# Second attention: one tile's projections, turns and relay moved one step forward on every engine

## What is computed

```python
q = (x @ Wq.T).reshape(B, S, 32, 16).transpose(0, 2, 1, 3)
k = _split_kv(x @ Wk.T, B, S)
v = _split_kv(x @ Wv.T, B, S)
q = q * cos + rotate_half(q) * sin
k = k * cos + rotate_half(k) * sin
scores = einsum('bhqd,bhkd->bhqk', q, k) / sqrt(16)
allowed = (j <= i) & (j > i - 128)
attn = softmax(where(allowed, scores, -inf))
out = einsum('bhqk,bhkd->bhqd', attn, v) @ Wo.T
x = layernorm(x + out)
```

## Time and profile before

| | |
|---|---|
| runs | 726.03, 734.14, 737.02 us (median 734.14) |
| the profiled execution | 728.87 us, its span 727.1 us |
| busy | PE 616.0 us (85%), DVE 393.3 (54%), ACT 270.3 (37%), POOL 238.9 (33%) |
| mean granted clock of TensorE | 0.911 |
| chain that ended last | PE 62%, DVE 10%, ACT 9%, DMA 7% |

### The profile page before, as it was taken

How to read it: one execution, slowest core, us unless ns; L and a number is a source line. 1 busy time by engine, 2 the same in 40 slices (tenths; PEclk the granted TensorE clock), 3 DMA queues, 4 the chain that set the end, 5 groups by cost and what they waited for, 6 DMA issues and landing times.

```text
span 727.1 us, 13453 instructions
## 1 busy us (share of the span) xinstructions
PE 616.0 (85%) x5108; PEld 482.4 (66%) x5108; DVE 393.3 (54%) x1126; ACT 270.3 (37%) x433; POOL 238.9 (33%) x348
## 2 busy tenths in 40 slices
PE   2998999669889787989989895868789799999984
PEld 2987976557667555666767673645458688888761
DVE  4325445697765774757777484552554243323264
ACT  5155045366654223334344342444430122221213
POOL 6002523543410245535444452362007311111071
PEclk9999999889999885999999897577799899999997
DMA  8921211342056425536272648020007759998465
GB/s 293 394 115 31 52 33 26 104 134 74 0 139 150 119 96 81 132 46 159 45 152 89 88 119 156 2 89 2 1 1 283 270 209 416 418 417 292 168 165 182
DMA packets 49455, 104.37 MB, mean 144 GB/s; under 512 B 12208, under 2 KB 18480, under 8 KB 47856
## 3 DMA queue, kind: packets, MB, share of 16 engines
q1 hardware_dynamic: 30032, 61.68, 24.0%
q0 software_dynamic: 13744, 31.61, 19.3%
q10 hardware_dynamic: 5616, 10.23, 3.9%
HBM read 63.77 MB, written 35.13 MB: 136 GB/s over the span
## 4 chain that ended last, share of the span: by engine, by line
PE 62%; DVE 10%; ACT 9%; issue 7%; DMA 7%; POOL 4%; SPq 1%; POOLq 0%; ACTq 0%; DVEq 0%
PE bank L332 20%; PE bank L515 10%; PE bank L368 9%; ACT FP L1451 4%; DVE FP L914 3%; PE bank L601 3%; PE bank L586 3%; PE bank L573 3%; DMA QS<-QS 2%; PE bank L750 2%; POOL FP L1866 2%; PE bank L716 2%; PE bank L391 2%; PE bank L546 1%; PE bank L379 1%
## 5 line engine op out<-in xcount | busy, mean ns | idle before, releaser
L1451 ACT ACTIVATE FP<-bank 128x512 f32<-128x512 f32 (+1 forms) x244 | 138.6, 611 | 311.3 <-PE bank L586 128.6
L1184 DVE CUSTOM_DVE_ANT_0 kraw<-bank,maskb 128x256 bf16<-128x256 f32 (+1 forms) x256 | 88.5, 401 | 58.0 <-PE bank L573 58.0
L515 PE MATMUL bank<-W,XR 128*128 128x512 f32 x348 | 104.1, 444 | 0.2
L332 PE MATMUL bank<-FP 128*128 128x128 f32 x558 | 87.3, 311 | 0.8 <-ACT FP L1451 0.8
L368 PE MATMUL bank<-W,XR 128*128 128x512 f32 x288 | 76.6, 415 | 5.2 <-DVE W L914 5.2
L515 PEld LDWEIGHTS bank<-W,XR 128*128 128x128 f32 x348 | 69.4, 211 | 16.0 <-DVE XR L914 0.8
L1818 POOL TENSOR_SCALAR_AFFINE_SELECT FP<-FP 128x512 f32<-128x512 f32 x64 | 41.4, 669 | 114.8 <-ACT FP L1451 114.8
L368 PEld LDWEIGHTS bank<-W,XR 128*128 128x128 f32 x288 | 63.7, 271 | 11.3 <-DVE W L914 5.6
L332 PEld LDWEIGHTS bank<-FP 128*128 128x128 f32 x558 | 65.1, 192 | 2.8 <-DVE FP L914 1.6
L332 PE MATMUL bank<-RP,W 128*128 128x512 f32 x192 | 48.8, 413 | 5.0 <-issue 2.8
L914 DVE TENSOR_TENSOR FP<-FP,bank 128x128 f32<-128x128 f32 (+1 forms) x39 | 14.4, 369 | 70.5 <-ACT FP L1451 44.9
(11 more groups left out here) (168 smaller groups left out, 1019.1 us busy)
## 6 DMA issues: line engine op xcount, KB each, us to landing
FP<-in_experts_dram SPq DMA_DIRECT2D x31, 768.0 KB, 6.6
slots_out<-QS SPq DMA_DIRECT2D x48, 256.0 KB, 2.6
FP<-slots_in POOLq DMA_DIRECT2D x31, 256.0 KB, 6.6
slots_out<-FP ACTq DMA_DIRECT2D x31, 256.0 KB, 7.7
slots_in<-RP SPq DMA_DIRECT2D x7, 1024.0 KB, 13.1
RP<-slots_out POOLq DMA_DIRECT2D x16, 384.0 KB, 5.7
QS<-slots_out POOLq DMA_DIRECT2D x10, 384.0 KB, 8.3
FP<-in_shared_dram SPq DMA_DIRECT2D x4, 768.0 KB, 8.0
```

The source lines that it names most:

```text
L332: mm = nc.tensor.matmul(bank, lhs, rhs, start=(n == 0), stop=(n == len(terms) - 1))
L515: mm = nc.tensor.matmul(b[:, :], *terms[n], start=(n == 0), stop=(n == len(terms) - 1))
L1184: ins = nc.vector.tensor_tensor_reduce(masked[:, 2 * (f % 2) + m, 0:n], b[:, m, :], maskb[:, m0:m0 + n], 1.0, -BIG, ALU.add, ALU.max, hmax ...
L1451: return nc.scalar.activation(o, i, func, **kw)
```

## The change

Each engine's order is changed, and nothing else. TensorE: the Q projection goes to step 0, and the K projection of tile t + 1 into step 7 of the iteration before; `turn_maxima(i, 1)` goes from step 1 to step 0; the turn of rotated K from 2 to 1, of rotated Q from 3 to 2, the V projection from steps 2 and 3 to 1 and 2; `turn_x(t + 1)` from step 6 to step 3. VectorE: `maxima_out(i, 1)` goes to step 0 and ahead of `rotate(t, 1)` and `rope_sum(t, 1)`, which go to step 0 too; the second rotation goes to step 1, the low parts to steps 1 and 2, the low part of the next x to step 3. ScalarE and GpSimd follow. SP is the same.

```diff
--- before.py
+++ after.py
@@ -641,16 +641,18 @@
                         key_scores(i, 2 * (s // 2), s % 2)
                     if s < 2 and d >= 0:
                         context_rows(U, d, s)
-                    if s < 2 and 2 <= t < T:
-                        project2(t, 1 - s)
-                    if s == 1 and i >= 0:
+                    if s == 0 and 2 <= t < T:
+                        project2(t, 0)
+                    if s == 0 and i >= 0:
                         turn_maxima(i, 1)
-                    if s == 2 and 2 <= t < T:
+                    if s == 1 and 2 <= t < T:
                         turn_rotated(t, 1)
                         project2(t, 2, 0, DC)
-                    if s == 3 and 2 <= t < T:
+                    if s == 2 and 2 <= t < T:
                         project2(t, 2, DC, 2 * DC)
                         turn_rotated(t, 0)
+                    if s == 3 and 2 <= t < T - 1:
+                        turn_x(t + 1)
                     if s == 4 and d >= 0:
                         turn_context(U, U, d)
                     if (i, s) == (-1, 0):
@@ -667,10 +669,10 @@
                         output(U, R, d, 0, DC)
                     if s == 6 and d >= 0:
                         output(U, R, d, DC, DC)
-                    if s == 6 and 2 <= t < T - 1:
-                        turn_x(t + 1)
                     if s == 7 and d >= 0:
                         output(U, R, d, 2 * DC, DC)
+                    if s == 7 and 1 <= t < T - 1:
+                        project2(t + 1, 1)
                     if i >= 0 and s in (3, 5, 7):
                         weigh(i, s // 2 - 1)
                 if i == T - 1:
@@ -1252,21 +1254,23 @@
                         row_maxima(r, s)
                     if s < 2 and d >= 0:
                         context_divided(U, d, s)
-                    if s == 1 and 2 <= t < T:
+                    if s == 0 and i >= 0:
+                        maxima_out(i, 1)
+                    if s == 0 and 2 <= t < T:
                         rotate(t, 1)
                         rope_sum(t, 1)
-                    if s == 1 and i >= 0:
-                        maxima_out(i, 1)
-                    if s == 2 and 2 <= t < T:
+                    if s == 1 and 2 <= t < T:
                         parts_low(t, 1)
                         rotate(t, 0)
                         rope_sum(t, 0)
+                    if s == 2 and 2 <= t < T:
+                        parts_low(t, 0)
                     if s == 3 and r < T:
                         maxima_split(r, 0)
                     if (i, s) == (-1, 3):
                         low_dense(("x2", 2), xa[2][1], xa[2][0])
-                    if s == 3 and 2 <= t < T:
-                        parts_low(t, 0)
+                    if s == 3 and 2 <= t < T - 1:
+                        low_dense(("x2", t + 1), xa[t + 1][1], xa[t + 1][0])
                     if s == 4 and d >= 0:
                         low_dense(("co", d), ca[1], ca[0])
                     if i == -1 and s in (2, 4, 5, 6):
@@ -1275,8 +1279,6 @@
                         maxima_out(r, 0)
                     if (i, s) == (-1, 6):
                         rates(slice(G, T), 4)
-                    if s == 6 and 2 <= t < T - 1:
-                        low_dense(("x2", t + 1), xa[t + 1][1], xa[t + 1][0])
                     if s == 7 and r < T:
                         maxima_split(r, 1)
                     if s == 7 and d >= 0:
@@ -1642,11 +1644,13 @@
                         context_out(d, 1)
                     if i >= 0 and (step % 2 == 0 or i >= 1):
                         weights_out(i, 2 * (step // 2), step % 2)
+                    if step == 1 and 2 <= t < T:
+                        parts_out_high(t, 1)
                     if step == 2 and 2 <= t < T:
-                        parts_out_high(t, 1)
-                    if step == 3 and 2 <= t < T:
                         values_out(t, ("qkv", t, 0))
                         parts_out_high(t, 0)
+                    if step == 3 and 2 <= t < T - 1:
+                        high_dense(("x2", t + 1), x2T[t + 1][:, 0])
                     if step == 4 and d >= 0:
                         high_dense(("co", d), coT[:, 0])
                     if (i, step) == (-1, 0):
@@ -1662,8 +1666,6 @@
                         high_part(15, 3, raw_c[3], wc_in[3])
                     if step == 6 and i >= 0:
                         context_out(i, 0)
-                    if step == 6 and 2 <= t < T - 1:
-                        high_dense(("x2", t + 1), x2T[t + 1][:, 0])
                     if i == T - 2 and step in (2, 5):
                         shared_high(step // 3)
                     if i == T - 1 and step == 2:
@@ -1838,11 +1840,11 @@
                         nc.gpsimd.memset(kS[:, 3].bitcast(F32), -1.0).then_inc(minus_ready, 1)
                     if i >= 0 and (step % 2 == 0 or i >= 1):
                         mask(i, 2 * (step // 2), step % 2)
-                    if step == 2 and i >= 0:
+                    if step == 1 and i >= 0:
                         stack_maxima(i, 1)
+                    if step == 3 and 2 <= t < T:
+                        stack_rows(t, 1)
                     if step == 4 and 2 <= t < T:
-                        stack_rows(t, 1)
-                    if step == 5 and 2 <= t < T:
                         stack_rows(t, 0)
                     if step == 6 and r < T:
                         stack_maxima(r, 0)
```

## The result

The changed kernel takes 749.66 us (747.16 to 752.93) against 734.92 us (726.03 to 737.02): 14.7 us more, a ratio of 1.0233 with a 95% interval of 1.0187 to 1.0280. The interval is clear of no change; whether the loss is over 2% it leaves open. The forecast was 742 us, +8, in a range of 727 to 757. The profiled execution has a span of 746.9 us, 19.8 more than the one before (727.1, at the fast end of its runs).

The account below looks back on a forecast made before the run. TensorE, busy 85% of the span, sets the pace. Iterations 1 to 4 +14.1, iteration 0 -4.4, iteration -1 +1, iteration 5 -2.7 make +8.0 us: 734.1 + 8 = 742 us, range 727 to 757.

Parts of the forecast that it names:

- K turn: TensorE's turn of rotated K, step 1: a new 3.5 us wait until 9.4, for VectorE's sum and context division.
- Q turn little earlier: TensorE's turn of rotated Q: at 13.8 us into the iteration against 14.38 now, 15.8 with the low clock.
- The relay: Delivery of each tile's stack, wanted by row_scores(r, 0): almost no gain from its start, in time only because iterations get longer.
- Iteration without the clock: Length of an iteration without a low-clock stretch behind the new wait: 33.65 us; 35.6 with one.
- the x turn's crowding of ring U: Four turns in four steps running through U's one bank: Q turn to maxima turn 7.0 us against 5.1.
- Clock: the step that failed: A low-clock stretch behind the 3.5 us wait in each iteration: 1.95 us reach the end, making 35.6 of 33.65.
- the wait of 1.88 us: Boundary wait of row_scores(r, 0) before the change, taken as once enough to bring low clock; cited against rival B.
- Iterations -1 and 0: Iteration -1 gets a projection, +1 us; iteration 0 swaps a slow projection and old waits for a 2.6 us wait, -4.4.
- Iteration 5: Its Q stack is sent 1.5 to 3 us sooner: about 36.2 us against 38.9, so -2.7.
- The other side: Case C, a gain: iterations at TensorE's own pace, every boundary wait gone, -20 us, 714; chance 0.07.
- Rival C: K turn doesn't wait, iterations take 29.6 us, boundary waits go: -20 us, 714; chance 0.07.
- Its deciding point: For C, VectorE's rotation, sum, row maxima and division must end by 5.9 us instead of 9.3.

## Why the prediction had the mechanism and missed the size

- **K turn.** Forecast: a wait of 3.5 us, K turn at 9.4, ended by the context division. Measured: 3.79, 9.58, ended by it. Right. The 0.3 us more is mostly the sum: 1.31 us to the next start instead of 0.92. GpSimd's masks ran beside it.
- **Q turn little earlier.** Forecast 13.8, or 15.8 with the low clock; measured 16.7 in iteration 3 and 17.4 in 2, 4 and 5. The relay gained nothing, as said, and the waits at the starts of iterations 2 to 5 went because the iterations got longer.
- **Iteration without the clock.** Forecast 33.65 us; with the wait filled, the mean of iterations 1 to 4 is 33.7. Right in sum, and wrong in the cause of one part: I laid 1.9 us on the x turn's crowding of ring U, and putting it back changed nothing. The Trainium skill says that a gap that repeats can mean too few buffers ("Perfetto Trace Analysis", Optimization Strategy; the prediction names a section next to it). The trace agrees at the K turn, where the division that drains the one bank came last (to 366.83; the sum was done at 364.84), and not in steps 3 to 5: with the x turn out of them TensorE waited as long, for row maxima.
- **Clock: the step that failed.** I took one low stretch of 3.7 to 4.3 us per iteration at half its length, 1.95 us that reach the end. It was 3.4 us once and 6.8 to 9.3 us in the other four. It cost 2.6 us an iteration behind the wait, and filling the wait took 3.3 off in all. The stretch of 4.3 us in the earlier trace rows was the wrong measure: it is the tail of a low stretch that had begun before its wait (the clock is 0.50 over 274.0 to 282.9 too), and that of 3.7 us follows two short waits, not a long one. Nor was the wait of 1.88 us enough by itself, as the prediction says it was: the clock was 1.00 over 316.3 to 317.5 behind it, and 0.50 over 318.8 to 321.5 only after another of 0.64. In sum, iterations 1 to 4 were forecast at +14.1 and came at +19.6; the clock's term was 7.8 of the 14.1, and 13.2 is what went when the wait was filled, so this term is 5.4 of the 5.5 that are missing there. The clock is low behind the wait in each of the five iterations, and 1.00 in each when the wait is filled. That it falls anew in each pass is what the Trainium skill ("TensorE: Matmul & The Clock Gate", HAM oscillation) says of such loops, and the trace agrees.
- **Iterations -1 and 0.** Forecast +1 and -4.4; measured +2.0 and -1.6. Both projections that moved there ran low: 4.52 us at 248.4 and 4.57 at 275.6 instead of 3.0, and a wait of 2.24 us stayed ahead of iteration 1.
- **Iteration 5.** Forecast -2.7; measured -0.8. Its Q stack was sent for 24.2 us in, not 20.5 to 22; the Q turn ahead of it came 17.4 us in, against 14.4 with the wait filled and the clock full. TensorE still waited 3.11 us, and 1.02 for the maxima's transfer.
- **The other side.** Rival C needed the K turn not to wait. It is what the K projection alone does, and that gave 715 us where C said 714. Its deciding point was the right one: VectorE's chain, which couldn't start before the maxima turn. Of this change C was wrong mainly because the eviction had been put ahead of the rotation; with the rotation first, a wait of 1.43 us and 720.92 us are left.

The profile's stretches add up: +2.0, -1.6, +19.6, -0.8 and +0.6 for all behind is 19.8 us. The sum of +8.0 was made from the profiled execution and has to answer to these 19.8, not to the 14.7 by which the medians differ; the profiled execution of before was a quick one of its kind. That 749.66 us lies inside 727 to 757 is in part luck. Of the 11.8 us missing, 5.5 are iterations 1 to 4 (the clock), 3.8 iterations -1 and 0, 1.9 iteration 5 and 0.6 the rest.

## What to carry to other kernels

When a schedule is moved forward as a block, the work that covered another engine's chain goes with it. Move the one product that fills a wait (here 17.5 us gained) and look at each engine's order for an operation that waits for a late partner ahead of one that is ready: moving one such call (the maxima eviction) behind the rotation was worth 29 us. Count a new wait on TensorE at its length and, if work at full clock follows, again at half the low stretch behind it (here 3.4 to 9.3 us of low clock, so an estimate of 1.7 to 4.7 us).

## What the runs showed of the hardware

- A wait of 3.8 us on TensorE was followed by work at the low clock in each of five iterations (3.4 us once, 6.8 to 9.3 us in the others). In three of the five the clock had fallen before the work resumed, with the last 0.9 to 1.6 us of the wait still to come; in the other two it fell 0.2 and 0.7 us after. With the turn of x put back all five low stretches had full length. Why one was short stays open.
- A wait of 1.35 to 1.43 us in the same place was followed by full clock in three of five. Filling 3.0 of the 3.8 us with discarded products kept it at 1.00 behind all five waits, and made the kernel faster by 12 us (ratios) to 15.6 (medians).
- The fetch of 2 x 384 KB took 13.0 to 13.2 us to landing with 1.7 MB of weights, gates and table sent at the same time, and 8.0 to 8.5 without (11.8 with them in the changed kernel; 9.8 without weights where it was sent one step sooner, right behind the K stack's).
- VectorE's add of two SBUF operands and GpSimd's masks get in each other's way: 1.47 and, for a pair of masks, 1.92 us side by side, 1.07 to 1.10 and 1.22 apart. In the kernel before, where the pair started some 0.5 us ahead of the add, the pair took 1.95 to 1.97 us and the add still 1.07 or 1.08. GpSimd in iteration 3 of the changed kernel, beside the add of 363.37:

```profile
363.29 1.92 POOL L1823 TENSOR_SCALAR_AFFINE_SELECT FP<-FP 128x512 f32<-128x512 f32 x2 [3.02 <-ACT FP L1453]
```
